# First attention of an audio tower: value products and output projection moved to other steps of a hand-written schedule

## The reference: what is computed

```python
h = h + _L0_attn_ref(_layernorm(h, axis=-1), L0_attn_Wq, L0_attn_bq, L0_attn_Wk, L0_attn_bk,
                     L0_attn_Wv, L0_attn_bv, L0_attn_Wo, L0_attn_bo)
```

## Time and profile before

| | before |
|---|---|
| time, median of 3 runs (lowest to highest) | 4313.74 us (4312.88 to 4317.17) |
| profiled execution: time / span | 4316.81 us / 4315.0 us |
| busy share of the span | PE 88%, DVE 66%, ACT 54%, POOL 46% |
| first and last value product of the stage | 194.0 us and 587.3 us |

### The profile page before, as it was taken

One profiled execution on the slowest core, in us unless ns is written; L12 is line 12 of the kernel. 1 busy time (PEld: TensorE's weight loads), 2 busy tenths in 40 slices (PEclk: granted clock), 3 DMA queues, 4 the chain that ended last, 5 costly groups with the idle time before them and its releaser, 6 DMA issues.

```text
span 4315.0 us, 110651 instructions
## 1 busy us (share of the span) xinstructions
PE 3815.2 (88%) x31697; PEld 2606.8 (60%) x31697; DVE 2862.9 (66%) x9352; ACT 2339.5 (54%) x5933; POOL 1974.2 (46%) x2276
## 2 busy tenths in 40 slices
PE   7488857697999799999897869999999999899999
PEld 7355533485666566666685546666666666555555
DVE  2577738785888644444465878888888887455554
ACT  5455525322444344444343548888888888455555
POOL 0143428674656412222474645555555555344333
PEclk9999967797999899999655879999999999999999
DMA  2111124331111323333112310000000001233332
GB/s 54 36 31 30 30 31 113 90 83 39 38 36 38 72 67 81 81 80 80 29 38 46 71 37 12 11 11 11 11 11 11 11 11 27 64 74 75 78 76 57
DMA packets 465512, 203.02 MB, mean 47 GB/s; under 512 B 435090, under 2 KB 455566, under 8 KB 465170
## 3 DMA queue, kind: packets, MB, share of 16 engines
q1 hardware_dynamic: 465298, 200.65, 20.5%
HBM read 154.67 MB, written 45.91 MB: 46 GB/s over the span
## 4 chain that ended last, share of the span: by engine, by line
PE 54%; issue 17%; POOL 14%; DVE 9%; SPq 2%; ACT 2%; DMA 2%; POOLq 0%; DVEq 0%; ACTq 0%
POOL att_P L3576 8%; PE sw_pH L4180 5%; PE moe_pH L2726 5%; PE sw_pY L4167 5%; PE moe_pY L2749 4%; DVE att_M L1177 3%; PE att_pS L982 3%; PE moe_pH L2730 3%; PE moe_pH L2736 2%; POOL att_norm_rstd L673 1%; PE att_pS L2219 1%; PE att_pO L1044 1%; PE ret_pR L1836 1%; PE att_pO L3039 1%; PE att_pP L3685 1%
## 5 line engine op out<-in xcount | busy, mean ns | idle before, releaser
L3576 POOL TENSOR_TENSOR att_P<-att_P,att_rden 125x498 f32<-125x498 f32 x512 | 520.3, 1016 | 514.6 <-DVE att_rden L3871 514.1
L3764 ACT ACTIVATE att_P<-att_Z,att_nb 125x249 f32<-125x249 f32 x1024 | 501.5, 494 | 22.4 <-DVE att_nb L3883 20.7
L2791 DVE TENSOR_TENSOR moe_hT<-moe_silu,moe_pH 128x498 f32<-128x498 f32 x384 | 258.8, 674 | 312.8 <-ACT moe_silu L2775 312.8
L4228 ACT ACTIVATE sw_hT<-sw_pH,sw_b 128x498 f32<-128x498 f32 x512 | 317.8, 672 | 220.9 <-PE sw_pH L4180 220.9
L3685 PEld LDWEIGHTS att_pP<-att_ident,att_P 124*125 124x125 f32 (+1 forms) x2048 | 262.6, 187 | 233.8 <-issue 233.8
L3685 PE MATMUL att_pP<-att_ident,att_P 124*125 124x124 f32 (+1 forms) x2048 | 349.8, 293 | 49.7 <-issue 28.9
L3883 DVE CUSTOM_DVE_ANT_0 att_Z<-att_pS,att_mask 125x249 f32<-125x249 f32 x1024 | 366.0, 413 | 29.9 <-PE att_pS L3673 27.9
L2775 ACT ACTIVATE moe_silu<-moe_pH 128x498 f32<-128x498 f32 x384 | 225.1, 586 | 263.0 <-PE moe_pH L2730 177.1
L3771 ACT ACTIVATE att_PTr<-att_pP 125x498 f32<-125x498 f32 x512 | 296.6, 579 | 102.2 <-PE att_pP L3685 94.7
L2702 POOL TENSOR_TENSOR moe_xe<-moe_share,moe_x 128x1992 f32<-128x1992 f32 x32 | 130.0, 4064 | 430.8 <-DMA moe_share<-mixing 380.5
L4087 POOL TENSOR_TENSOR sw_acc<-sw_acc,sw_Z 128x249 f32<-128x249 f32 x224 | 154.1, 688 | 365.2 <-DVE sw_Z L4307 364.4
(11 more groups left out here) (463 smaller groups left out, 9697.2 us busy)
## 6 DMA issues: line engine op xcount, KB each, us to landing
moe_share<-mixing SPq DMA_DIRECT2D x64, 498.0 KB
sw_share<-mixing SPq DMA_DIRECT2D x64, 498.0 KB, 5.5
ffn_W<-in_ffn_pairs SPq DMA_DIRECT2D x64, 192.0 KB, 2.4
att_F<-h_stream SPq DMA_DIRECT2D x192, 62.5 KB
att_X<-h_stream SPq DMA_DIRECT2D x192, 62.5 KB
h_stream<-att_H SPq DMA_DIRECT2D x64, 62.5 KB
ffn_F<-h_stream SPq DMA_DIRECT2D x64, 62.5 KB
ret_F<-h_stream SPq DMA_DIRECT2D x64, 62.5 KB
```

The lines of the kernel that those rows point to most:

```text
L3576: g.tensor_tensor(own, own, bc(rden[:, j % 2, c, :], T), ALU.mult).then_inc(*scaled.one())
L3764: ins = a.activation(P[:, r, c, t, :], Z[:, r, c, t, :], ACT.Exp, scale=-1.0, bias=nb[:, r, c, t:t + 1], accum_out=den[:, r, c, t:t + 1])
L4228: a.activation(hT[:, k % 4, :, :], pH[:, place, :, 0:T], ACT.Relu, bias=b1[:, k:k + 1]).then_inc(*hid_ready.one())
```

## The change

It moves instructions between steps and changes two waits that depend on the order. No instruction is added or taken away. On PE the values stand with turn A (step 3), the outputs' turns at step 5, back at step 7, y at step 1 of the next slot together with the sum of the pair before, and the rows' turns at step 1. The core of the diff, with the ACT and DVE parts and the new `sum_up` and `take`:

```diff
@@ POOL
 def pre(n, u, step):
-    if step == 3:
+    if step == 1:
         g.wait_ge(*xn_ready.before(n))
         norm.center(g, n, g4(F[:, u % 2, :, :, :]))
+    if step == 6:
+        norm.power(g, n)
 def proj(n, u, step):
     if step == 0:
-        norm.power(g, n)
         g.wait_ge(*xT_done.before(n))
...
 def ends(n, u, step):
-    if step == 2:
+    if step == 4:
         g.wait_ge(*mean_done.before(n))
...
         tail.square(g, n)
-    if step == 6:
+    if step == 7:
         tail.power(g, n)
...
@@ PE
 def proj(n, u, step):
-    if step == 3:
+    if step == 1:
         pe.wait_ge(*xn_ready.after(n))
         pe.wait_ge(*xT_ready.before(n))
-        if since(n, 3):
-            pe.wait_ge(*OT_ready.after(n - 3))
+        if since(n, 4):
+            pe.wait_ge(*OT_ready.after(n - 4))
         st.held(pe)
...
 def post(n, u, step):
-    if step == 1:
+    if step == 3:
         pe.wait_ge(*exp_ready.after(n))
         pe.wait_ge(*OT_ready.before(n))
-        pe.wait_ge(*xT_ready.after(upto(n + 2)))
+        pe.wait_ge(*xT_ready.after(upto(n + 3)))
         st.held(pe)
...
         ins.then_inc(*o_done.one())
-    if step == 3:
+    if step == 5:
         pe.wait_ge(*OT_ready.after(n))
...
         ins.then_inc(*turned.one())
-    if step == 5:
+    if step == 7:
         pe.wait_ge(*ob_ready.after(n))
...
         ins.then_inc(*back.one())
-    if step == 7:
+
+def sum_up(n):
+    pe.wait_ge(*tail.powered.after(n))
+    st.held(pe)
+    for t in range(2):
+        ins = pe.matmul(pX[:, 256:258],
+                        tail.xc[0:ROWS[t], 2 * t:2 * t + 2, :].rearrange("p g c -> p (g c)"),
+                        tail.rstd[0:ROWS[t], 2 * t:2 * t + 2], start=(t == 0), stop=(t == 1))
+    ins.then_inc(*mean_done.one())
+
+def ends(n, u, step):
+    if step == 1:
         pe.wait_ge(*oT_ready.after(n))
...
         ins.then_inc(*y_done.one())
+        if since(n, 1):
+            sum_up(n - 1)
 def sums(n, u, step):
-    if step == 1:
-        pe.wait_ge(*tail.powered.after(n))
+    if step == 1 and isinstance(n, int) and n == PAIRS - 1:
+        pe.wait_ge(*h_ready.after(n))
         pe.wait_ge(*mean_ready.before(n))
-        pe.wait_ge(*h_ready.after(upto(n + 1)))
-        st.held(pe)
-        for t in range(2):
-            ins = pe.matmul(pX[:, 256:258],
-                            tail.xc[0:ROWS[t], 2 * t:2 * t + 2, :].rearrange("p g c -> p (g c)"),
-                            tail.rstd[0:ROWS[t], 2 * t:2 * t + 2], start=(t == 0), stop=(t == 1))
-        ins.then_inc(*mean_done.one())
-waves(pe, (nothing, proj, front, main, post, nothing, sums), STEPS, PERIOD)
+        sum_up(n)
+waves(pe, (nothing, proj, front, main, post, ends, sums), STEPS, PERIOD)
...
@@ ACT
 def pre(n, u, step):
-    if step == 5:
+    if step == 3:
         norm.square_scalar(a, n)
...
 def post(n, u, step):
-    if step == 1:
+    if step == 3:
         a.wait_ge(*o_done.after(n))
...
             *OT_ready.one())
-    if step == 5:
+    if step == 7:
         a.wait_ge(*back.after(n))
...
+def take(n):
+    a.wait_ge(*mean_done.after(n))
+    a.activation(mean[:, bass.ds(n * 2, 2)], pX[:, 256:258], ACT.Copy,
+                 scale=1.0 / T).then_inc(*mean_ready.one())
+
+def ends(n, u, step):
+    if step == 3 and since(n, 1):
+        a.wait_ge(*h_ready.after(n))
+        take(n - 1)
+
 def sums(n, u, step):
-    if step == 1:
-        a.wait_ge(*mean_done.after(n))
-        a.activation(mean[:, bass.ds(n * 2, 2)], pX[:, 256:258], ACT.Copy,
-                     scale=1.0 / T).then_inc(*mean_ready.one())
-waves(a, (pre, proj, nothing, main, post, nothing, sums), STEPS, PERIOD)
+    if step == 3 and isinstance(n, int) and n == PAIRS - 1:
+        take(n)
+waves(a, (pre, proj, nothing, main, post, ends, sums), STEPS, PERIOD)
...
@@ DVE
 def pre(n, u, step):
-    if step == 3:
+    if step == 1:
         v.wait_ge(*loaded.after(n, u % 2))
         norm.sums(v, n, g4(F[:, u % 2, :, :, :]))
-    if step == 7:
+    if step == 5:
         norm.spread(v, n, 1e-5)
...
 def proj(n, u, step):
-    if step == 3:
+    if step == 1:
         v.wait_ge(*xT_done.after(n))
...
 def post(n, u, step):
-    if step == 3:
+    if step == 5:
         v.wait_ge(*turned.after(n))
...
 def ends(n, u, step):
-    if step == 0:
+    if step == 2:
         v.wait_ge(*y_done.after(n))
+        if since(n, 1):
+            v.wait_ge(*mean_done.after(n - 1))
         v.wait_ge(*stored.lagging(n, u % 2))
...
             *h_ready.one())
-    if step == 1:
+    if step == 3:
         v.wait_ge(*h_ready.after(n))
         tail.sums(v, n, g4(H1[:, u % 2, :, :, :]))
-    if step == 5:
+    if step == 6:
         tail.spread(v, n, 1e-5)
```

## The result

The changed kernel takes 4267.97 us (median of 4 runs, 4267.50 to 4274.38), the kernel before, run beside it, 4315.30 (4312.88 to 4317.17): a ratio of 0.9894, with an interval of 0.9877 to 0.9911. It is faster by 47 us where 28 were forecast, and lies 9 us under the range. The profiled execution is the longest of the four: 4274.38 us, with a span of 4272.6.

What follows compares the result with a forecast made beforehand. The prediction took PE's waits on the one score buffer, no engine full, as the bound; 0.99 us less a slot in 28 slots (27.7 us) plus 1 in the four before gave 4286 us, range 4277 to 4302.

Steps and rivals of the forecast that it cites:

- The main gain: On PE at turn A: its 1.04 us wait for the maxima would be covered by 1.83 us of values.
- What is late next: On DVE between M2 and M3: its work there would make M3 0.39 us late, with PE's wait moving to G0.
- M1 late by 0.30: On DVE before M1: M1 would start at 4.29 us, 0.30 behind G1's scores, which are ready at 3.99.
- The sum on PE at 0.50: On PE between G0 and G1: the sum was priced at 0.50 us of that gap's 1.73 us of work.
- The loop's branch at nothing: One slot in four: the branch falls into PE's 1.11 us wait and costs nothing; uncovered, up to 0.09 a slot.
- The first slots and the end: Four slots before s = 6 would gain 1 us in all; the last pair's chain to its mean stays the same.
- All behind the store at nothing: After the token mean's store: no gain was counted; the stage's 28.7 us was taken off the whole program's time.
- The rule on the pipe: On DVE from M2 to M3: whole durations would make the stretch 0.08 us longer and the slot 11.84, not 11.76.
- 1, the likeliest: The stage's slot falls to 11.6 to 12.1 us, the program to 4277 to 4296 us; chance 0.70.
- 2: DVE, late at M1 and M3, takes a good part back: slot 12.06 to 12.36, 4294 to 4303 us; chance 0.17.
- 3: The wait for the maxima merely moves from turn A to G0, so no gain: 4305 to 4322 us; chance 0.07.
- 4: POOL's queue of norm power, tail power and scaling delays sum and rows' turns, so slower: 4323 us; chance 0.06.

Runs made afterwards that it cites:

- e1: The changed kernel with the rows' turns and all that belongs to them back at their old place; 4303.50 us, ratio 0.9958.
- e2: The kernel before with only the rows' turns and the work ahead of them moved two steps sooner; 4321.78 us, ratio 1.0012.
- e8: The changed kernel with the tail's spread moved behind M3 and the sum put behind the rows' turns; 4269.61 us, ratio 0.9890.
- e6: The changed kernel with three small DVE operations added between M3 and the next M0; 4272.44 us in one execution.
- e5: The changed kernel with three small DVE operations added between M2 and M3; 4267.70 us in one execution.
- e11: The changed kernel with 60 chained DVE reductions between the last token mean and its store; 4312.16 us, ratio 0.9991.

## Why the prediction was right in its mechanism and wrong in its time

**The main gain: right.** Turn A's 1.04 us wait was to be covered by the values; it is (403.69, no idle), and PE's list has no wait of turn A left. e1 and e2 add what I had not worked out: the outputs' part alone leaves the rows' turns behind the values and pays 0.54 for pO, so only both together give the 1.33 a slot (12.74 to 11.41).

**What is late next: right in place, too large.** The step that failed is the term "What is late next is thus DVE between M2 and M3", in its size: 0.39 was 0.14. Its parts, as the changed kernel shows them: the scaling holds DVE 0.33 (406.73 to 407.06), not 0.39; a spread's small operation 0.08 to 0.10 (407.51 to 407.59), not 0.18. I had taken the 0.18 from a row whose next instruction was H, at 408.51 in the earlier trace rows. H has waits of its own, and in the changed kernel too it starts 0.25 behind the small operation ahead of it (401.61 to 401.86), so it is no measure of how long such an operation holds the engine; what holds H there the rows don't say. These sizes made M2 to M3 2.87 for 3.09. The range's low edge had named the right cause, neighbours on DVE that overlap more than I took, but went to a slot of 11.6 only.

**M1 late by 0.30: too large as well.** It is 402.20 - 402.02 = 0.18 late, H to M1 being 0.34, not 0.44, and the values hide it: turn A could start at 402.20 + 1.41 = 403.61 and starts at 403.69.

**The sum on PE at 0.50: too large.** It is 0.37 (399.69 to 400.06), turn B 0.25 for 0.35, while rows to G1 is 0.50 for 0.34. The first gap is 2.70 for 2.78. The old 0.50 came from a row in which the sum stood behind a wait; that this made it longer is likely and not shown.

**The sum over the slot.** By the four gaps, 11.76 was too long by 0.08, 0.03 and 0.25, and too short by 0.03: 11.43, the slot shown. The mean of 24 slots is 11.41.

**The loop's branch at nothing: wrong, and small.** It shows in one slot in four at M3 to M0: 2.80 against 2.61, and at M1 to M2 of the slot behind it, 3.06 against 2.96: together 0.07 a slot. Before, it was 0.33 at M3 to M0 and 0.11 at M2 to M3, 0.11 a slot. G0 starts at 398.11, where M3's start at 396.49 + 1.41 = 397.90 would have let it. The 1.11 us of wait that were to cover the branch are not there in full: G0 starts 1.47 behind v (396.64 to 398.11), where 1.74 was forecast. That 1.74 would have covered the branch is worked out and not tested.

**The first slots and the end.** From M0 of s = 6 to M0 of s = 33 the stage gains 343.85 - 307.93 = 35.9 us where 27 x 0.99 = 26.7 were forecast; the slots before, 1.2 for 1; from there to the store 2.6 for 1. Together 39.7 for 28.7. So 11 of the 18 us by which the forecast missed are in the stage, 9 of them from the slot. With the whole stage right the forecast would have been some 4275, still 7 us above the median.

**All behind the store at nothing.** These 7 us are the second step that failed: the prediction took the gain of the stage for the gain of the program and put what lies behind the store at nothing, without a reason. It measures 7.6 us less (3706.8 for 3714.4); whether that is an effect of the change or scatter stays open, as said above.

**The rule on the pipe.** The Trainium skill, "VectorE: DVE Perf Modes", section "The DRAIN you can't avoid", has the next operation wait until the pipe is empty, from which the prediction estimated a slot of 11.84; it left out what the same section adds: "A next op that is not held starts earlier". This case's trace goes with that addition: in the changed kernel the operation behind a 0.42 us one starts 0.33 after its start (406.73 to 407.06), the one behind a 0.17 us one 0.08 to 0.10 after, and the one that needs the result of the operation ahead a full length behind (407.06 to 407.51, 0.45 behind 0.41).

**The rivals.** 1, the likeliest, has the right course, but its slot of 11.6 to 12.1 was missed too. 2 and 3 are out: M3 is 0.14 late and not 0.7, no gap moved back. 4 did not happen here; e8 shows its place to be real. POOL's powers stay at 1.01 and 1.02 us beside a busy DVE, so no power was lengthened by the lock on the port that the Trainium skill, "SBUF — State Buffer", section "Who interferes with whom", describes. The third small operation of e6, 0.59 us long next to POOL's scaling where those of e5 take 0.16, fits such a lock, with DVE as the one that waits; no run tests it on its own. The error was one-sided: I priced lateness with care and held the other side to 11.6.

## What to carry to other kernels

How long an operation holds its engine is read where the next one was free to start; a row whose next instruction waits for something else gives an upper bound, and such bounds added up in a chain made the forecast's gain too small, 0.99 a slot where it was 1.33. When a wait can be covered by moving a long block into its gap, look at once at who shares the block's output buffer: here one part of the change was worth 10 us in the stage, the other cost 6, and both together gained 40. After such a move the slack is uneven: find the gap that an engine holds by little (0.14 us), take that off, and look in the queue of the engine whose work was moved.

## What the runs showed of the hardware

- Small DVE operations on 125x4 that need nothing of one another cost 0.07 us each in a busy stretch (e5: 0.21 for three), though a row gives one 0.16 to 0.17.
- Next to POOL's scaling one such operation takes 0.59 us (e6), and ends within 0.03 us of the scaling's end.
- In the stage, with PE busy 93%, the granted clock is 1.00, the level of 2.4 GHz. Behind the store, where PE is busy 147 of 251 us, it lies between the two levels and differs from run to run. The first 250 us there (columns as in the earlier trace rows) in the changed kernel, then in e5:

```profile
559.40:810.00 250.60, 146.92 (x686) 84.60 (x687) 171.69 (x509) 100.51 (x267) 158.20 (x204) 0.66 0.40 91
```

```profile
566.50:816.00 249.50, 140.72 (x739) 85.38 (x739) 172.82 (x520) 103.03 (x271) 163.33 (x212) 0.73 0.41 93
```

The mean granted clock is 0.66 and 0.73 for the same code, and e5 gets further in the same time (739 matmuls for 686). That goes with e5's short part behind the store, 3699.4 against 3713.2. The same tendency shows over the 37 executions of the kernel before that ran beside e1 to e11 (4309.27 to 4324.96 us): the one with the lowest granted clock over the whole program, 0.923, takes 4323.71, and the three with the highest, 0.929, take 4309.27 to 4315.17. Which of the two, the clock or the time, is the cause no run tells.
